# A twelve-layer decoder kernel: features made with their projection, two VectorE operations fewer per unit of best places, a three-step root refinement, a longer two-bank start, and a weight load moved

## The reference

```python
q = (jax.nn.elu(q) + 1.0) * scale
k = jax.nn.elu(k) + 1.0
```

```python
topv, topi = jax.lax.top_k(scores, K_TOP)
probs = jax.nn.softmax(topv, axis=-1)
attn = jnp.zeros_like(scores).at[bi, hi, ti, topi].set(probs)
attn_mean = attn.mean(axis=1)
V = x_vision @ Wv
c_t = jnp.einsum('btg,bgd->btd', attn_mean, V)
```

```python
sim = (sim - mean) * ATTN_MATRIX_SCALE + mean
attn = jax.nn.softmax(sim, axis=-1)
out = jnp.einsum('hij,hjd->hid', attn, vh)
```

## Time and profile before

| | |
|---|---|
| median of 3 runs | 4182.41 us (4179.08 to 4185.37) |
| the profiled execution | 4179.52 us, of which its span is 4177.4 us |
| PE busy | 3278.6 us (78%) |
| VectorE busy | 3025.4 us (72%) |
| ScalarE busy | 1873.8 us (45%) |
| GpSimd busy | 434.0 us (10%) |
| TensorE clock granted, mean | 0.872 |
| DMA | 69.04 MB, mean 17 GB/s |

### The profile page before, as it was taken

How to read it: one execution, slowest core, us unless ns; L and a number is a source line. 1 busy time by engine, 2 the same in 40 slices (tenths; PEclk the granted TensorE clock), 3 DMA queues, 4 the chain that set the end, 5 groups by cost and what they waited for, 6 DMA issues and landing times. The chain is left out here.

```text
span 4177.4 us, 68244 instructions
## 1 busy us (share of the span) xinstructions
PE 3278.6 (78%) x28617; PEld 1810.8 (43%) x28626; DVE 3025.4 (72%) x4043; ACT 1873.8 (45%) x2125; POOL 434.0 (10%) x255
## 2 busy tenths in 40 slices
PE   6799999999999955777775886666654669378579
PEld 3444444444444424344433755322322347244357
DVE  4478888888888876699996465699997544546542
ACT  2266666666666632344442242344442236145233
POOL 0000000000000000100000313144341000000000
PEclk9799999999999978799997998656667889599789
DMA  2000000000000000100001101000000110000010
GB/s 85 9 16 9 9 16 9 9 10 15 9 9 16 1 7 7 26 15 9 9 1 72 54 2 49 1 0 0 0 0 0 42 41 1 19 31 1 1 42 6
DMA packets 21635, 69.04 MB, mean 17 GB/s; under 512 B 5201, under 2 KB 5713, under 8 KB 20434
## 3 DMA queue, kind: packets, MB, share of 16 engines
q1 hardware_dynamic: 21330, 64.69, 5.3%
HBM read 49.07 MB, written 0.52 MB: 12 GB/s over the span
## 5 line engine op out<-in xcount | busy, mean ns | idle before, releaser
L1231 PE MATMUL banks<-L0x_ring,L0x_context_rows 32*101 32x512 f32 x6400 | 736.4, 592 | 7.3 <-ACT L0x_ring L1280 3.4
L1218 PE MATMUL banks<-L0x_q_thirds,L0x_context_thirds 32*128 32x512 f32 x4800 | 584.1, 593 | 11.4 <-ACT L0x_ring L1291 6.0
L1291 ACT COPY L0x_ring<-banks 128x1024 f32<-128x1024 f32 (+1 forms) x416 | 387.2, 982 | 407.8 <-PE banks L1218 407.8
L1231 PEld LDWEIGHTS banks<-L0x_ring,L0x_context_rows 32*101 32x101 f32 x6400 | 304.6, 163 | 394.4 <-issue 378.2
L1332 DVE TENSOR_TENSOR L0x_ring<-L0x_ring,L0x_greatest 128x2048 f32<-128x2048 f32 (+1 forms) x208 | 468.6, 2267 | 1.5
L1280 ACT ACTIVATE L0x_ring<-L0x_ring 128x2048 f32<-128x2048 f32 (+1 forms) x208 | 385.4, 1853 | 81.1 <-DVE L0x_ring L1332 80.7
L1348 DVE TENSOR_TENSOR L0x_maxima<-L0x_maxima,L0x_ring 128x1024 f32<-128x1024 f32 (+1 forms) x288 | 322.4, 1161 | 118.0 <-ACT L0x_ring L1291 117.9
L1218 PEld LDWEIGHTS banks<-L0x_q_thirds,L0x_context_thirds 32*128 32x128 f32 x4800 | 266.1, 186 | 284.8 <-issue 257.3
L1810 ACT ACTIVATE L1x_probs<-banks 128x2048 f32<-128x2048 f32 (+1 forms) x112 | 196.6, 1755 | 252.1 <-PE banks L1744 210.0
L1869 DVE TENSOR_REDUCE L1x_maxima<-banks 128x3 f32<-128x1203 f32 (+1 forms) x176 | 241.4, 1373 | 31.2 <-PE banks L1702 30.9
L1892 DVE SCALAR_TENSOR_TENSOR L1x_probs<-L1x_probs,L1x_floor 128x1024 f32<-128x1024 f32 (+1 forms) x208 | 252.2, 1216 | 11.4 <-ACT L1x_probs L1810 11.1
(11 more groups left out here) (959 smaller groups left out, 5385.7 us busy)
## 6 DMA issues: line engine op xcount, KB each, us to landing
L0x_q_thirds<-L0x_q_context SPq DMA_DIRECT2D x180, 64.0 KB, 2.0
L1f_expert_weights<-in_L1f_experts SPq DMA_DIRECT2D x16, 512.0 KB, 9.9
L2f_expert_weights<-in_L2f_experts SPq DMA_DIRECT2D x8, 512.0 KB, 5.9
L3a_expert_weights<-in_L3a_experts SPq DMA_DIRECT2D x8, 512.0 KB, 5.0
L3f_expert_weights<-in_L3f_experts SPq DMA_DIRECT2D x8, 512.0 KB, 5.6
L1x_k<-L1x_k_rows SPq DMA_DIRECT2D x64, 50.0 KB
L0x_context_thirds<-in_context_thirds SPq DMA_DIRECT2D x1, 2496.0 KB, 14.5
L1x_context<-in_context SPq DMA_DIRECT2D x4, 600.4 KB, 5.3
```

The lines of the kernel that those rows point to most:

```text
L1218: mm = pe.matmul(k.ps[:, score_bank(s) + i, :], thirds[group_rows(i), slot, t, :], q_thirds[group_rows(i), u // 2 % 2, t, :], start=t == 0 ...
L1231: mm = pe.matmul(k.ps[0:CW, 4 + r, :], rows1[group_rows(r), j, :], ring[group_rows(r), s % RING, i, :], start=s == FIRST[u] and i == 0, st ...
L1291: act.copy(ring[0:r, s % RING, 2 * p:2 * p + len(pair), :], k.ps[0:r, bank:bank + len(pair), :]).then_inc(copied, 1)
```

## The change

Five edits. (1) `refine_root` has three operations for four. (2) `ALONE` goes from 8 to 10. (3) `elu_columns` takes the place of the projection and `elu_plus_one`: ScalarE makes relu(-a) straight from PSUM and its exponential with scale -1, VectorE adds max(a, 0) straight from PSUM. (4) In best places minus the maximum is made by ScalarE before its exponentials, and the division by the number of heads moves into the copy of the result. (5) The load of L2_ffn's weights is issued in the stage of best places, not in the one that opens L2_xattn.

```diff
 def refine_root(dve, step, root, value, work):
-    step(dve.tensor_tensor(work, value, root, ALU.mult))
-    step(dve.tensor_tensor(work, work, root, ALU.mult))
-    step(dve.tensor_scalar(work, work, -0.5, 1.5, ALU.mult, ALU.add))
-    step(dve.tensor_tensor(root, root, work, ALU.mult))
+    step(dve.scalar_tensor_tensor(out=work, in0=root, scalar=-0.5, in1=root, op0=ALU.mult, op1=ALU.mult))
+    step(dve.tensor_tensor(work, work, value, ALU.mult))
+    step(dve.scalar_tensor_tensor(out=root, in0=work, scalar=1.5, in1=root, op0=ALU.add, op1=ALU.mult))
...
-    def use(self, layer):
+    def use(self, layer, later=False):
...
-                if ahead and HOME[ahead] != HOME[layer]:
+                if ahead and HOME[ahead] != HOME[layer] and not later:
                     self.load(sp, ahead)
...
-ALONE = 8
+ALONE = 10
...
+def elu_columns(k, jobs, low, own_rows, scale, values):
+    items = [(job, half) for job in jobs for half in range(2)]
     with k.stage() as (block, signal):
+        product, lowered, exped, taken, cleared, risen = (signal() for _ in range(6))
+        def part(a, half):
+            return a[:, half * 512:(half + 1) * 512]
+        @block.gpsimd
+        def _(pool):
+            values.clear(pool, cleared)
+        @block.tensor
+        def _(pe):
+            for n, ((dst, w, own), half) in enumerate(items):
+                if n >= 8:
+                    pe.wait_ge(taken, n - 7)
+                pe.matmul(k.ps[:, n % 8, :], w, part(k.zT, half), start=True, stop=True).then_inc(product, 1)
         @block.scalar
         def _(act):
+            def negative_part(n):
+                act.wait_ge(product, n + 1)
+                act.activation(part(low[:, n // 2, :], n % 2), k.ps[:, n % 8, :], ACT.Relu, scale=-1.0).then_inc(lowered, 1)
+            negative_part(0)
+            for n in range(len(items)):
+                if n + 1 < len(items):
+                    negative_part(n + 1)
                 act.wait_ge(lowered, n + 1)
-                act.activation(low[:, n, :], low[:, n, :], ACT.Exp).then_inc(exped, 1)
+                a = part(low[:, n // 2, :], n % 2)
+                act.activation(a, a, ACT.Exp, scale=-1.0).then_inc(exped, 1)
         @block.vector
         def _(dve):
+            for n, ((dst, w, own), half) in enumerate(items):
                 dve.wait_ge(exped, n + 1)
+                o = part(dst, half)
+                dve.scalar_tensor_tensor(out=o, in0=k.ps[:, n % 8, :], scalar=0.0, in1=part(low[:, n // 2, :], half),
+                                         op0=ALU.max, op1=ALU.add).then_inc(taken, 1)
+                if own:
+                    dve.wait_ge(taken, n + 1)
+                    dve.tensor_scalar(o, o, own_rows, scale, ALU.mult, ALU.mult).then_inc(risen, 1)
...
+            @block.sync
+            def _(sp):
+                k.weights.load(sp, "L2_ffn")
...
+                    act.activation(nmax[:, n % 2:n % 2 + 1], top[:, n % 2, 0:1], ACT.Copy, scale=-1.0).then_inc(negated, 1)
+                    act.wait_ge(negated, n + 1)
                     act.activation(ea[:], sc[:, n % 2, :], ACT.Exp, bias=nmax[:, n % 2:n % 2 + 1])
...
                 def scale(n):
                     dve.wait_ge(exped, n + 1)
                     d = den[:, n % 2:n % 2 + 1]
-                    step(dve.tensor_scalar(d, d, float(H), None, ALU.mult))
                     dve.reciprocal(d, d).then_inc(recip, 1)
...
-                    dve.tensor_copy(ct[:, g, :], k.ps[:, 6, 0:P]).then_inc(stored, 1)
+                    dve.tensor_scalar(ct[:, g, :], k.ps[:, 6, 0:P], 1.0 / H, None, ALU.mult).then_inc(stored, 1)
...
-                        if r == 0:
-                            step(dve.tensor_scalar(nmax[:, n % 2:n % 2 + 1], top[:, n % 2, 0:1], -1.0, None, ALU.mult))
...
-        w = k.weights.use("L2_xattn")
+        w = k.weights.use("L2_xattn", later=True)
```

More of the change, by code:

```diff
@@ L2232, in _ @@
             act.activation(dst[:], src[:], func)
-def elu_plus_one(k, a, low, own_rows, scale):
-    first, second = a
+def elu_columns(k, jobs, low, own_rows, scale, values):
+    items = [(job, half) for job in jobs for half in range(2)]
     with k.stage() as (block, signal):
-        lowered, exped, risen = signal(), signal(), signal()
-        parts = [(t, g) for g in range(4) for t in (first, second)]
+        product, lowered, exped, taken, cleared, risen = (signal() for _ in range(6))
[10 more added lines that the diff above has]
+                pe.matmul(k.ps[:, n % 8, :], w, part(k.zT, half), start=True, stop=True).then_inc(product, 1)
@@ L2245, in _ @@
         @block.scalar
         def _(act):
-            for n, (t, g) in enumerate(parts):
+            def negative_part(n):
[5 more added lines that the diff above has]
+                    negative_part(n + 1)
                 act.wait_ge(lowered, n + 1)
-                act.activation(low[:, n, :], low[:, n, :], ACT.Exp).then_inc(exped, 1)
+                a = part(low[:, n // 2, :], n % 2)
+                act.activation(a, a, ACT.Exp, scale=-1.0).then_inc(exped, 1)
@@ L2251, in _ @@
         @block.vector
         def _(dve):
-            for n, (t, g) in enumerate(parts):
-                dve.tensor_scalar(low[:, n, :], t[:, g, :], 0.0, None, ALU.min).then_inc(lowered, 1)
-            for n, (t, g) in enumerate(parts):
+            for n, ((dst, w, own), half) in enumerate(items):
                 dve.wait_ge(exped, n + 1)
-                dve.scalar_tensor_tensor(out=t[:, g, :], in0=t[:, g, :], scalar=0.0, in1=low[:, n, :], op0=ALU.max, op1=ALU.add).then_inc(risen, 1)
-                if t is first:
-                    dve.wait_ge(risen, n + 1)
-                    dve.tensor_scalar(t[:, g, :], t[:, g, :], own_rows, scale, ALU.mult, ALU.mult)
+                o = part(dst, half)
[4 more added lines that the diff above has]
+                    dve.tensor_scalar(o, o, own_rows, scale, ALU.mult, ALU.mult).then_inc(risen, 1)
@@ L2354, in layer1_attention @@
         values = ValueRows(v, d)
-        linear_columns(k, [(dst[:, g, :], [(w[n][:, g * P:(g + 1) * P], k.zT)], None, 1.0, None)
-                           for g in range(G) for n, dst in (("q", q), ("k", kk))], values)
-        elu_plus_one(k, (q, kk), low, w["own"], d ** -0.5)
+        elu_columns(k, [(dst[:, g, :], w[n][:, g * P:(g + 1) * P], n == "q") for g in range(G) for n, dst in (("q", q), ("k", kk))],
+                    low, w["own"], d ** -0.5, values)
         values.fill(k, [(k.zT, w["v"])], H)
@@ L3586, in best_places @@
             scored, copied, topped, exped, left, weighed, taken, recip, turned, moved, summed, stored = (signal() for _ in range(12))
-            projected, placed = signal(), signal()
+            projected, placed, negated = signal(), signal(), signal()
+            @block.sync
+            def _(sp):
+                k.weights.load(sp, "L2_ffn")
             def height(j):
```

## The result

The changed kernel takes **4131.75 us** (median of 4 runs, 4130.57 to 4138.99) beside 4181.32 for the kernel before, timed with it: a ratio of 0.9883, interval 0.987 to 0.9895, so 44 to 54 us less. It is faster, as forecast, but by more: 4142.5 was predicted with a range down to 4136, so about 10 us of gain were not in the sum.

A forecast was written before the change was run, and what follows sets the result against it. It saw no single bound: TensorE in all places, VectorE in best places, engine chains elsewhere. Gains of 4.9 + 7.3 + 12.3 + 11.9 + 3.1 = 39.5 us from 4182.4 gave 4142.9, stated as 4142.5, range 4136 to 4153.

The forecast's parts named there:

- Root refinement, 4.9: In the norms' VectorE chains, one operation fewer in each of 24 counted calls gains 4.9 us, from 4.0 to 5.2.
- 25 calls lose one operation each: 25 x 0.20: In the norms and three other places, each shortened VectorE chain saves one 0.20 us step: 5.0 us before excluding one call.
- ALONE, 7.3: At the start of all places, two TensorE waits go and `values` begin at 233.75, not 241.09: 7.3 us, from 4.0 to 7.5.
- The second rival: Start of all places: half clock or another wait leaves 4.0 us, and the instruction stop stays; total 4148.5, chance 0.15.
- signs of being wrong: Features pair over 1.3 us, the 3 us stop staying or moving to best places, or low TensorE clock after 230 us.
- One idle gap of 2 us did not slow slot 8: Start of all places: with only one idle gap left, TensorE was expected to keep full clock, supporting 7.3 us.
- Features, 12.3: In L1_attn's features, overlapping the projection, with ScalarE pairs of 1.02 us as the bound, gains 12.3 us.
- The first rival: In L1_attn's features, ScalarE pays more per instruction: 1.56 us a pair, gain 4.3, total 4151; chance 0.09.
- Best places, 11.9: In best places, 63 VectorE operations of 0.19 us leave the path, ScalarE's cost mostly hidden: 11.9 us, from 10.5 to 12.2.
- Weight load, 3.1: At the opening of L2_xattn, moving the load saves 0.8 us of issue and 2.3 of TensorE's stop: 3.1 us.
- Instructions of this dense piece may still be a little late, so 2.3: In L2_xattn's 256 small products, only 2.3 us of the 3.11 us TensorE stop was counted as removed.
- Range: Whole kernel: 4138 to 4150 us with chance 0.71 if all edits stay within bounds; 4136 to 4153 with two rivals included.

The follow-up runs named there:

- padded: The changed kernel with a fourth step, a multiplication by 1, added to the new root refinement, restoring its length; 4146.29 us (ratio 0.9922).
- filler_more: The changed kernel plus unused TensorE matmuls in three normalisations ahead of the L2 feed-forward and three more in layer 3; 4124.17 us (ratio 0.988).

## Why the prediction was right or wrong

- **Root refinement, 4.9: the step that failed.** "25 calls lose one operation each: 25 x 0.20" is right as a chain (VectorE's start times in the two traces step by 0.20 at each call). The step took for granted that TensorE's stages behind a norm keep their length. They do not: with the root edit taken away from the changed kernel the tail goes from 979.6 to 989.5, 9.9 us, of which 13 x 0.20 = 2.6 are chain. The other 7.3 stand for the most part at operations that read what TensorE has made, and its busy time in the tail is 714.70 us in the one and 708.15 in the other for the same work, so I put them down to its clock. The trace's record of the granted clock has 303.8 us at half clock in the tail of both profiles of before, 307.2 without the root edit, and 283.3 in both of the changed kernel and with the root edit alone. In all, the term was worth 11.7 (taken from the full change) to 14.3 (alone) by medians. (Two slips of the sum beside it matter little: 24 x 0.20 is 4.8 and not 4.9, and the two new operations would have to cost 0.10 more each, not 0.07, to eat the gain of a call.)
- **ALONE, 7.3:** the waits right, 6.3 by the rows. Two waits went and slot 9 ran at full clock, but slot 10, behind the one pause left, ran at half: 4.55 us where the sum has 2.7, and `values` began at 235.28. "One idle gap of 2 us did not slow slot 8" did not carry over to slot 10. This was no chance: in all eleven profiles with `ALONE` = 8 slot 8 takes 2.85 or 2.86 us, and in all eight with 10 that keep the wait slot 10 takes 4.54 to 4.56; and slot 10 took 4.55 before, too, a row that the prediction did not read. The second rival named this, but left the edit a gain of 4.0, and it had 6.3. Of the signs of being wrong, a low clock behind 230 us came: it is 0.89 from 225 to 240 us, half from 231.1 on.
- **Features, 12.3:** 12.5; the last feature was forecast 22.8 us after the columns' copy and came after 22.56. The pair of ScalarE operations was 1.02 in the sum and is 0.99 to 1.00. The first rival (1.56 a pair) did not show. The Trainium skill ("ScalarE: Activation LUTs", Rules for kernel authors) gives its 0.3 us plus 0.83 ns per element for an ACTIVATE whose bias is a 128x1 operand. The estimate from it, 0.72 for each and 1.45 a pair, passed over that condition: the rows of this pair show no such operand. One operation takes 0.64 to 0.72 us here, and the pair 0.99, since neighbours overlap.
- **Best places, 11.9:** the stretch gave 12.1, with the context's projection in it, whose clock moves by chance (546.37 and 543.66 for one kernel). The unit shrank by 0.36, and the 31 of the earlier trace rows by 11.2 (489.3 to 478.1). ScalarE's small operation took 0.20 and stayed hidden: 2.1 us are left between the divisor and its use.
- **Weight load, 3.1:** 4.1 in the run with it alone. "Instructions of this dense piece may still be a little late, so 2.3" was too careful: of 3.11 us, 0.17 stay with the load alone moved and 0.31 in the changed kernel. That the load caused the stop is shown; that it was the fetch of instructions is my reading of "issue". The Trainium skill ("Runtime: NRT & Kernel Launch", Instruction fetch mechanics) says that crossing a block is mostly hidden. If the stop was a fetch, that fits the trace only once the transfer is away.
- **Range:** it took in bounds of each chain, and none for TensorE's clock outside the edited stages, although the profile had shown a mean of 0.872 with half clock in many stages. A bound of 7.3 us below, known only now, would have held the result.

Why the shorter chain changes the clock I can say only in part. Shown is: in the tail the three-step chain gives 978.5 to 979.7 us and the four-step chain 988.4 to 989.6 (985.4 once), and it is the chain's length and not its operations (padded); work of TensorE in the pause can do the same without any shorter chain (981.66 in the kernel before); and with four calls shortened, 0.8 us of chain, the tail was 3.3 shorter, in one profile; this alone proves little, since features alone had 3.0 less without an edit there. A fifth step did not make the tail longer, so the relation is no straight line. How the chip decides stays open.

## What to carry to other kernels

In this kernel a microsecond taken off a chain between two dense pieces of TensorE was worth two to four, and one added cost nothing in the tail: the piece behind it runs at full or at half clock, and small shifts decide which. So sum such an edit as chain plus a clock term with a bound of its own on either side (here 2.6 and +7.3 over 13 calls), and before explaining a rest, profile the same program twice and compare stretches between fixed operations. In a pause that cannot be removed, unused matmuls into a free bank can hold the clock, but each place has to be tried: three places gave 7 us, all places together nothing. And a single profile proves little: `filler_more`, with no filler between L1_attn's products and best places, took 1009.1 us there, where the other changed kernels without one took 1013.4 to 1014.9.

## What the runs showed of the hardware that was not expected

- One program, two profiles: the 26 products of the context's projection took 5.19 and 3.11 us, only by the clock. The tail behind best places was the same to 0.2 us in both.
- With one chain step of 0.2 us taken out, the tail was 981.5 us in one execution and 988.6 in another.
- An operation of 0.2 us added to 25 calls (about 5 us of chain) cost 3.0 us by medians (interval 0 to 7), and nothing in the tail.
- With a weight load just ahead (359 GB/s from 2607 to 2609 us) TensorE stopped for 3.11 us without any semaphore, and for 2.53 to 3.14 us in every profile with the load there; with the load elsewhere 0.04 to 0.41 us were left.
